# Last causal attention with keys on partitions: exponentials of turned scores, row maxima from separate scores, row- and column-tiled products

## The reference

```
h = _rmsnorm(x, g1)
c = h @ w_down
q = _rope(split(c @ wq), pos)
k = _rope(split(c @ wk), pos)
v = split(c @ wv)
scores = jnp.einsum('bhqd,bhkd->bhqk', q, k) / jnp.sqrt(jnp.float32(HD))
scores = jnp.where(causal, scores, -jnp.inf)
attn = jax.nn.softmax(scores, axis=-1)
o = jnp.einsum('bhqk,bhkd->bhqd', attn, v).transpose(0, 2, 1, 3).reshape(b, s, L)
x = x + o @ w_up
```

## Time and profile before

| | us |
|---|---|
| median of 3 runs | 2549.88 |
| lowest and highest run | 2538.66, 2573.20 |
| span of the profiled execution | 2550.4 |
| PE busy in it (share of the span) | 2276.2 (89%) |
| DVE, ACT, POOL busy in it | 1837.0, 1048.9, 1060.3 |

### The profile page before, as it was taken

One profiled execution on the slowest core, in us unless ns is written; L12 is line 12 of the kernel. 1 busy time (PEld: TensorE's weight loads), 2 busy tenths in 40 slices (PEclk: granted clock), 3 DMA queues, 4 the chain that ended last, 5 costly groups with the idle time before them and its releaser, 6 DMA issues. The chain is left out here.

```text
span 2550.4 us, 43889 instructions
## 1 busy us (share of the span) xinstructions
PE 2276.2 (89%) x12444; PEld 1771.8 (69%) x12476; DVE 1837.0 (72%) x3856; ACT 1048.9 (41%) x3603; POOL 1060.3 (42%) x1087
## 2 busy tenths in 40 slices
PE   5899995389999999994999999959899999479998
PEld 3677774267777777763999999924577777357776
DVE  5788886868888888877666666642456565679887
ACT  1688882222222222222665655601354544222222
POOL 2433332255666665643333333342322222356664
PEclk9899997589999999996999999965699999589999
DMA  5000000000000000000000000000000000010001
GB/s 103 3 0 0 0 0 1 1 29 15 15 1 15 15 15 15 1 0 3 5 3 4 3 3 4 2 0 0 1 0 0 0 0 0 1 30 15 15 1 33
DMA packets 34033, 22.40 MB, mean 9 GB/s; under 512 B 11056, under 2 KB 30640, under 8 KB 33936
## 3 DMA queue, kind: packets, MB, share of 16 engines
q1 hardware_dynamic: 30912, 20.19, 3.1%
q10 hardware_dynamic: 3024, 1.08, 0.2%
HBM read 19.16 MB, written 2.10 MB: 8 GB/s over the span
## 5 line engine op out<-in xcount | busy, mean ns | idle before, releaser
L77 POOL TENSOR_TENSOR b_moe_hid_low<-b_moe_hid,b_moe_hid_high 128x512 fp32r<-128x512 f32 x256 | 333.5, 1303 | 238.5 <-DVE b_moe_hid_high L72 233.1
L920 ACT ACTIVATE b_moe_silu<-bank 128x512 f32<-128x512 f32 x256 | 153.5, 600 | 455.2 <-PE bank L84 449.9
L1458 POOL TENSOR_TENSOR c_prob<-c_prob,c_recip 128x480 f32<-128x480 f32 x128 | 126.3, 987 | 306.3 <-DVE c_recip L1609 306.3
L1567 ACT ACTIVATE c_prob<-bank,c_shift 128x120 f32<-128x120 f32 x512 | 178.0, 360 | 180.3 <-DVE c_shift L1601 180.3
L549 ACT ACTIVATE dt_prob<-bank,dt_shift 128x128 f32<-128x128 f32 x512 | 146.4, 368 | 187.8 <-DVE dt_shift L574 187.3
L941 DVE TENSOR_TENSOR b_moe_gu<-bank,b_moe_silu 128x512 f32<-128x512 f32 x256 | 175.9, 687 | 62.0 <-PE bank L84 53.6
L77 POOL TENSOR_TENSOR e_moe_hid_low<-e_moe_hid,e_moe_hid_high 128x512 fp32r<-128x512 f32 x128 | 166.6, 1302 | 106.9 <-DVE e_moe_hid_high L72 105.3
L72 DVE CAST c_ts_high<-bank 128x480 fp32r<-128x480 f32 x128 | 84.9, 663 | 163.6 <-PE bank L1489 163.6
L945 DVE TENSOR_TENSOR b_moe_hid<-bank,b_moe_gu 128x512 f32<-128x512 f32 x256 | 176.9, 691 | 8.8
L574 DVE TENSOR_REDUCE dt_shift<-bank 128x4 f32<-128x512 f32 x128 | 88.0, 687 | 125.7 <-PE bank L84 125.7
L549 ACT ACTIVATE a_att_prob<-bank,a_att_shift 128x120 f32<-128x120 f32 x512 | 177.4, 368 | 0.0
(11 more groups left out here) (354 smaller groups left out, 6315.2 us busy)
## 6 DMA issues: line engine op xcount, KB each, us to landing
X<-in_x SPq DMA_DIRECT2D x4, 512.0 KB, 8.8
b_moe_w_gate<-in_b_wgT SPq DMA_DIRECT2D x8, 256.0 KB, 2.9
b_moe_w_up<-in_b_wuT SPq DMA_DIRECT2D x8, 256.0 KB, 3.3
b_moe_w_down<-in_b_wdT SPq DMA_DIRECT2D x8, 256.0 KB, 3.4
out<-X SPq DMA_DIRECT2D x8, 256.0 KB, 2.4
a_cs<-in_ctxT SPq DMA_DIRECT2D x8, 180.0 KB, 2.5
c_cs<-in_ctxT SPq DMA_DIRECT2D x32, 45.0 KB, 1.7
b_moe_sel<-in_sel SPq DMA_DIRECT2D x8, 128.0 KB, 3.5
```

Of the source, the lines that this page charges most:

```text
L77: return eng.tensor_tensor(low.bitcast(F32R), x, high, ALU.subtract)
L920: act.activation(act_s[j % 2][:], gate_b[j % 2][:], ACT.Silu).then_inc(s_silu, 1)
L1458: pool.tensor_tensor(prob[k][:], prob[k][:], recip[:, k, :].unsqueeze(2).broadcast_to([P, HG, NKV]), ALU.mult).then_inc(s_norm, 1)
L1567: i = act.activation(prob[k][:, h, :], score_b[g % 2][:, h * NKV:(h + 1) * NKV], ACT.Exp, bias=shift[:, k, h:h + 1], accum_out=sums[:, k, ...
```

## The change

`attend_turned` takes the place of `attend` in the last stage. It works in rounds, one batch's worth of each step per round. Names that follow: `scores` are taken as before, in two pairs of groups that share two banks, and only for the row maxima. `mz` gets the maxima as high and low parts, TensorE turns it, and VectorE spreads it with `maxsel` (`mrow`). `turned_scores` makes the scores again with the keys on partitions: `ks` is the stationary operand, `qd` the spread queries, the causal mask goes in turned, and a product of ones with `mrow` adds the negated maxima. So the exponentials of a group are one instruction of 512 columns without a bias, and need no transposes. `values` multiplies them with a `vh` of 32 columns a head (8 values, a column of ones, zeros), each of a group's four heads into its own 32 output partitions. ScalarE copies the bank (`outs`), TensorE turns it back, VectorE divides by the denominators, TensorE turns `heads`, ScalarE copies it, and one projection with a `d_up8` of 128 rows follows. Products that lie in different 32-row strips stand next to each other in TensorE's stream. At the start of the kernel, `d_up8` is one load, padded on the host.

```diff
+        maxsel = sb("maxsel", [P, HG])
...
-                            ("d_v", [LAT, LAT]), ("d_router", [D, E1])):
+                            ("d_v", [LAT, LAT]), ("d_up8", [D, D]), ("d_router", [D, E1])):
...
-        d_up8 = sb("d_up8", [64, 2, D])
...
+                load(sp, maxsel[:], consts["maxsel"], s_load)
...
-                sp.wait_ge(s_zrow, 1)
-                for i in range(8):
-                    load(sp, d_up8[8 * i:8 * i + 4], w["d_up"].rearrange("(p i d) n -> i d p n", p=2, i=8)[i], s_load)
...
-                pool.memset(d_up8[:], 0.0).then_inc(s_zrow, 1)
...
+        def attend_turned(tag, ctx, QT, KT, V, wo, dst):
...
+            qs = [[f32(f"qs_{part}{i}", [P, P]) for part in ("high", "low")] for i in range(4)]
+            kd = [[f32(f"kd_{part}{i}", [P, HG, P]) for part in ("high", "low")] for i in range(2)]
+            qd = [[f32(f"qd_{part}{i}", [P, HG, P]) for part in ("high", "low")] for i in range(2)]
+            vh = [f32(f"vh{i}", [P, H, 32]) for i in range(2)]
+            negmax = [f32(f"negmax{i}", [P, H]) for i in range(2)]
+            mz = [f32(f"mz{i}", [P, P]) for i in range(2)]
+            mrow = [f32(f"mrow{i}", [P, HG, P]) for i in range(2)]
+            ones_r = f32("ones_r", [P, P])
+            probT = [[f32(f"probT{i}{g}", [P, HG * P]) for g in range(NG)] for i in range(2)]
+            outs = [f32(f"outs{i}", [P, NG * P]) for i in range(2)]
...
+            score_b, turned_b, out_b, side_b = bank[0:2], bank[2:6], bank[6], bank[7]
...
+            def over_rounds(eng, body):
+
+                for t in range(4):
+                    body(t, t)
+                with stepped(eng, 4, NB - 4, 4) as t:
+                    for k in range(4):
+                        body(t + k, k)
+                for t in range(NB - 4, NB + 3):
+                    body(t, t % 4)
...
+                    def spread(b, v):
+                        u = v % 2
+                        pool.wait_ge(s_cast, b + 1)
+                        keep_low(pool, ks[v][1][:], KT[:, bass.ds(b * P, P)], ks[v][0][:])
+                        keep_low(pool, qs[v][1][:], QT[:, bass.ds(b * P, P)], qs[v][0][:]).then_inc(s_lowk, 1)
+                        pool.wait_ge(s_lowk, b + 1)
+                        wait(pool, s_score, 2 * b - 2)
+                        for part in range(2):
+                            i = pool.tensor_tensor(kd[u][part][:].bitcast(F32R), ks[v][part][:].unsqueeze(1).broadcast_to([P, HG, P]),
+                                                   headsel[:].unsqueeze(2).broadcast_to([P, HG, P]), ALU.mult)
+                        i.then_inc(s_kd, 1)
+                        wait(pool, s_turned, 4 * b - 4)
+                        for part in range(2):
+                            i = pool.tensor_tensor(qd[u][part][:].bitcast(F32R), qs[v][part][:].unsqueeze(1).broadcast_to([P, HG, P]),
+                                                   headsel[:].unsqueeze(2).broadcast_to([P, HG, P]), ALU.mult)
+                        i.then_inc(s_qd, 1)
+                        wait(pool, s_pv, b - 1)
+                        pool.tensor_copy(vh[u][:, :, 0:8],
+                                         V[:, bass.ds(b * P, P)].rearrange("p (h d) -> p h d", h=H)).then_inc(s_vprep, 1)
+
...
+                    def scores(b, v, pair):
+                        u = v % 2
+                        if pair == 0:
+                            pe.wait_ge(s_kd, b + 1)
+                        wait(pe, s_max, 2 * b + pair)
+                        groups = (2 * pair, 2 * pair + 1)
+                        for g in groups:
+                            pe.matmul(score_b[g % 2][:], ident16[:], causal16[:].rearrange("p h k -> p (h k)"),
+                                      start=True, stop=False)
+                        for qp, kp in ((0, 0), (0, 1), (1, 0)):
+                            for g in groups:
+                                rows = group_rows(g)
+                                i = pe.matmul(score_b[g % 2][:], qs[v][qp][rows, :].bitcast(F32R),
+                                              kd[u][kp][rows].rearrange("p h k -> p (h k)").bitcast(F32R),
+                                              start=False, stop=(qp == 1))
+                        i.then_inc(s_score, 1)
+
+                    def turned_scores(b, v):
+                        u = v % 2
+                        pe.wait_ge(s_qd, b + 1)
+                        wait(pe, s_exp, 4 * b)
+                        for g in range(NG):
+                            pe.matmul(turned_b[g][:], causal16[:, 0, :],
+                                      ident16[:].unsqueeze(1).broadcast_to([P, HG, P]), start=True, stop=False)
+                        for kp, qp in ((0, 0), (0, 1), (1, 0)):
+                            for g in range(NG):
+                                rows = group_rows(g)
+                                pe.matmul(turned_b[g][:], ks[v][kp][rows, :].bitcast(F32R),
+                                          qd[u][qp][rows].rearrange("p h q -> p (h q)").bitcast(F32R),
+                                          start=False, stop=False)
+                        pe.wait_ge(s_mrow, b + 1)
+                        for g in range(NG):
+                            rows = group_rows(g)
+                            pe.matmul(turned_b[g][:], ones_r[rows, :].bitcast(F32R),
+                                      mrow[u][rows].rearrange("p h q -> p (h q)").bitcast(F32R),
+                                      start=False, stop=True).then_inc(s_turned, 1)
+
+                    def values(b, v):
+                        u = v % 2
+                        pe.wait_ge(s_vprep, b + 1)
+                        wait(pe, s_heads, b)
+                        for g in range(NG):
+                            pe.wait_ge(s_exp, 4 * b + g + 1)
+                            for j in range(HG):
+                                i = pe.matmul(out_b[32 * j:32 * j + 32, g * P:(g + 1) * P], vh[u][:, HG * g + j, :],
+                                              probT[u][g][:, j * P:(j + 1) * P], start=True, stop=True)
+                        i.then_inc(s_pv, 1)
+
+                    def body(t, v):
+                        if has(t - 1):
+                            pe.wait_ge(s_mz, 2 * t)
+                            wait(pe, s_out, t - 3)
+                            pe.transpose(side_b[:, 0:P], mz[(v - 1) % 2][:], ident[:]).then_inc(s_mt, 1)
+                        if has(t):
+                            scores(t, v, 0)
+                        if has(t - 3):
+                            pe.wait_ge(s_heads, t - 2)
+                            if has(t - 1):
+                                pe.wait_ge(s_mrow, t)
+                            pe.transpose(side_b[:, P:2 * P], heads[(v - 3) % 2][:], ident[:]).then_inc(s_ht, 1)
+                        if has(t - 2):
+                            values(t - 2, (v - 2) % 4)
+                        if has(t):
+                            scores(t, v, 1)
+                        if has(t - 3):
+                            pe.wait_ge(s_headT, t - 2)
+                            pe.matmul(side_b[:, 2 * P:2 * P + D], headT[(v - 3) % 2][:], wo[:], start=True,
+                                      stop=True).then_inc(s_y, 1)
+                        if has(t - 1):
+                            turned_scores(t - 1, (v - 1) % 4)
+                        if has(t - 2):
+                            pe.wait_ge(s_outs, t - 1)
+                            for g in range(NG):
+                                i = pe.transpose(out_b[:, g * P:(g + 1) * P], outs[(v - 2) % 2][:, g * P:(g + 1) * P], ident[:])
+                            i.then_inc(s_back, 1)
+                    over_rounds(pe, body)
...
+                def _(act):
+                    def body(t, v):
+                        if has(t - 3):
+                            act.wait_ge(s_ht, t - 2)
+                            act.activation(headT[(v - 3) % 2][:], side_b[:, P:2 * P], ACT.Copy).then_inc(s_headT, 1)
+                        if has(t - 2):
+                            act.wait_ge(s_pv, t - 1)
+                            act.activation(outs[(v - 2) % 2][:], out_b[:], ACT.Copy).then_inc(s_outs, 1)
+                        if has(t - 1):
+                            u = (v - 1) % 2
+                            wait(act, s_pv, t - 2)
+                            for g in range(NG):
+                                act.wait_ge(s_turned, 4 * (t - 1) + g + 1)
+                                act.activation(probT[u][g][:], turned_b[g][:], ACT.Exp).then_inc(s_exp, 1)
+                    over_rounds(act, body)
...
+                    def high_parts(b, v):
+                        wait(dve, s_turned, 4 * b - 12)
+                        keep_high(dve, ks[v][0][:], KT[:, bass.ds(b * P, P)])
+                        keep_high(dve, qs[v][0][:], QT[:, bass.ds(b * P, P)]).then_inc(s_cast, 1)
+                    high_parts(0, 0)
+                    high_parts(1, 1)
...
```

(39 more changed lines are left out.)

69 lines of the change are left out of this document (65 added, 4 removed).

## The result

The changed kernel takes 2443.6 us (median of four runs, 2434.2 to 2458.9) where the kernel before, run beside it, took 2544.3 (2531.9 to 2573.2). The ratio is 0.967, with a 95% interval from 0.963 to 0.972: faster by 3.3%. A second set on another occasion gave 2438.1 us and 0.966 (0.961 to 0.971). The forecast was 2440 us, in a range of 2425 to 2515.

What follows compares the result with a forecast made beforehand. The last attention was bound by TensorE's stream; changed, a chain of waits sets rounds of 7.5 us for 11.08. Stage end 2062.6 against 2172.0: 2550.4 - 109.4 - 0.6 = 2440 us, range 2425 to 2515.

Steps and rivals of the forecast that it cites:

- Sum 7.07: TensorE's own work in one round of the last causal attention: 7.07 us, where it was 11.08.
- 7.34: Chain of waits through the first pair's maxima, which sets a round of the last attention: 7.34 us.
- 7.5: Forecast round of the last attention: the chain's 7.34 us plus 0.2 for the restart behind the wait.
- the 0.2 for the restart: 0.2 us a round added for TensorE's restart behind its wait for the maxima.
- 0.89 or 3.56 us: Value passes of a round: 0.89 us if column strips run side by side, 3.56 one after the other; 0.89 taken.
- the rival's 9.74 us a round: Value passes in column strips don't overlap: round 9.74 us plus 0.2, kernel 2513 us; chance 0.10.
- They cost nothing until the values pass 1.43: Transpose of the heads and values (0.12 + 1.16 us) lie in TensorE's 1.55 us wait for the maxima.
- The exclusion of VectorE and GpSimd: A VectorE cast or the split may wait up to 1.03 us for GpSimd; costs nothing up to 0.9.
- I let the clock rise by then: Start of the last attention: half clock through round 2, which takes 13.1 us, so to 1833.6 us.
- the drain: Last attention's end: three rounds without scores, 5 + 4.5 + 2 = 11.5 us as an estimate.
- Rival 3: TensorE stays at 1.2 GHz through the last attention: 5.8 us more a round, kernel 2616 us; chance 0.09.
- at most 0.6 us with GpSimd late next: Kernel start: TensorE begins up to 2.8 us earlier, but GpSimd's last cast limits the gain to 0.6 us.

Runs made afterwards that it cites:

- two of the reordered kernels: Changed kernel with second pair and turned scores in one 32-row stretch: 2514.5 us; same with the maxima's transpose behind the first pair: round 7.69 us.

## Why the prediction was right, step by step

**The round.** "Sum 7.07", then "7.34" for the chain, then "7.5" with a restart. Measured 7.32, and 7.33 in most rounds. From the starts in the timeline: first pair to the transpose of the heads 1.42 (said: 1.42), second pair 1.43 (1.42), values 1.08 by the row (the first start to the last, 1911.41, is 0.81, and the last pass 0.27; said 0.89, and 0.27 for the form), projection 0.33 (0.22), turned scores 2.09 (2.11), output transposes 0.49 (0.50). The step that was too large is the 0.2 for the restart: TensorE goes on at 1911.79, 0.05 us after the maxima end at 1911.74, with nothing behind it. That the chain's sum without it came out within 0.02 us is in part luck: the two maxima take 1.29 where I put two durations, 1.38, and the projection 0.33 for 0.22. The terms that were differences of starts in the earlier trace rows, the two pairs, the turned scores and the output transposes, are each right to 0.02. In the mean over the stage the loop's end gives half of it back: 7.39, 29 x 7.39 = 214.3 where I had 217.5.

**Column strips.** The least known term, 0.89 or 3.56 us, went to the low end, by the earlier trace rows. Those rows show row strips, so this was a choice by likeness that turned out right, not a reading. Exchanging the loops brings back 1.38 us and no more; the rival's 9.74 us a round assumed strictly serial passes.

**What hides the values.** "They cost nothing until the values pass 1.43" leaves 0.27 of cover. Measured it is 0.18: with 1.38 us more of values the round grew by 1.20, and with the projection in that place it shrank by 0.19.

**The others' load.** VectorE 4.97 us a round (5.1), ScalarE 2.94 (3.5; its exponentials follow each other 0.5 us apart, not 0.614), GpSimd 5.20 (5.3). The exclusion of VectorE and GpSimd is there (0.57 for a cast of 0.17) and has its cover, as said; two of the reordered kernels lack it.

**The start.** First product at 1800.73 (said 1801), round 0 of 8.9 us (8.7). The mis-sized step is the clock: "I let the clock rise by then", at 1833.6; it rose at 1820.3, as the third round began. The second round took 10.7 us (10.8 said), the third 7.1 instead of 13.1. The stage ended at 2053.5 against 2062.6: 6.2 us of that are this step, 3.2 the 29 rounds, and the drain took 0.3 more than I gave it. Rival 3, TensorE held at 1.2 GHz, did not come: TensorE was busy 13.5 of 19 us of mostly 32-row products ahead of the rise.

**Kernel start.** Said at most 0.6 us with GpSimd late next; got 0.4, and GpSimd is late: TensorE starts 0.94 earlier, GpSimd's last cast of the block ends at 36.02 and the next stage begins at 36.31. What was wrong is why TensorE starts earlier: not because there are fewer loads, but because another one is last in the list.

**The total.** The profiled executions differ by 8 us more than forecast: the stage ended 9.1 us earlier than said, and the stages behind it took 1 us more than I let them. That the median of 2443.6 lies within 4 us of 2440 is partly chance, since the changed kernel's profiled execution (2434.2) is the fastest of its four, and that of the kernel before (2550.4) took longer than the median beside it, 2544.3.

## What to carry to other kernels

Cost a stream of matmuls by differences of start times between neighbours of the same kind, and a change of form as a term of its own (0.27 to 0.3 us here); such a sum gave TensorE's own stream as 7.07, and with its waits gone it measured 7.14; the margin added for a restart was the error. Maxima that follow each other cost less than their durations (1.29 for two of 0.69). When a chain and an engine's own sum lie within 0.3 us, look for a step that can move into the chain's wait: that, one stretch less and two tiny steps left out were worth 0.56 us of 7.39 a round. Before an order takes the cover off a small step, look at what that step shares with another engine: here a step of 0.17 us took up to 0.96, close to GpSimd's longest operation of 1.04.

## What the runs showed of the hardware

- **TensorE goes ahead across strips.** Products of a free row or column strip start before older ones of a busy strip: twelve products issued group by group start in fours, and the next column strip begins while three of eight passes of the one before are still to start.
- **A wait of one kernel's round can halve the clock.** In one order TensorE stood idle 1.47 us a round for VectorE, the granted clock was 0.50 for 3.4 of every 10.2 us, and the same order without that wait had rounds of 7.03 at 1.00. Elsewhere in the round 1.31 us of idle time did not lower the clock.
- **The spread between the profiles is clock, in stages that the change does not touch.** (The other runs have only a mean clock; the kernel before ran 2518 us at 0.930 and 2583 at 0.902.) In the profiles, the first attention has a stretch at 0.50 that lasts 17 to 68 us, and the start of the last attention moves with it, from 1793.8 to 1820.3 (the changed kernel at 1795.6 had 20.5 us of it, the one without the split at 1820.3 had 68.3). The stage just ahead stood at 0.50, and did so for 140 to 157 us on end and into ours, in every profile but one, that of the kernel with the maxima taken twice:

```profile
1675.00:1706.00 31.00, 4.16 (x11) 1.82 (x11) 16.35 (x58) 1.28 (x2) 21.76 (x12) 0.51 0.00 0
1706.00:1758.00 52.00, 48.31 (x166) 22.87 (x166) 25.72 (x38) 13.73 (x22) 21.61 (x16) 1.00 0.00 0
```

There 52 us of it ran at 1.00, the last attention began at 1758.8, and the kernel with the longer round (8.53 us) took 2436.4 us, as long as the changed one. What tips that stage one way or the other was not tried.
